# Masks laid into the score banks by ScalarE and VectorE, three pairs of banks, and statistics spread over the loop

## Time and profile before

| | |
|---|---|
| Time, median of 3 runs | 558.53 us (557.37 to 559.1) |
| The profiled execution: its own time, and its span | 557.49 us, 555.7 us |
| TensorE busy | 511.4 us (92%) |
| VectorE busy | 409.1 us (74%) |
| GpSimd busy | 377.6 us (68%) |
| ScalarE busy | 318.3 us (57%) |
| The first `scores` | starts at 23.96 us |
| The first `transpose_max` (line 1115) | starts at 34.25 us |
| The last `transpose_max` | starts at 378.67 us |
| Mean granted TensorE clock | 0.945 |

### The profile page before, as it was taken

One profiled execution on the slowest core, in us unless ns is written; L12 is line 12 of the kernel. 1 busy time (PEld: TensorE's weight loads), 2 busy tenths in 40 slices (PEclk: granted clock), 3 DMA queues, 4 the chain that ended last, 5 costly groups with the idle time before them and its releaser, 6 DMA issues.

```text
span 555.7 us, 19805 instructions
## 1 busy us (share of the span) xinstructions
PE 511.4 (92%) x6899; PEld 414.2 (75%) x6900; DVE 409.1 (74%) x1373; ACT 318.3 (57%) x750; POOL 377.6 (68%) x865
## 2 busy tenths in 40 slices
PE   3778999999999999999999999998898999999990
PEld 1346777877777777777777777776747999999990
DVE  3368666688898888887776766776667888888970
ACT  1415556666566657575666566455207777777760
POOL 8774365667878777778788787776621666665663
PEclk8757999999999999999999999999588999999996
DMA  6910423111111202201111112000122222222210
...
DMA packets 53445, 34.49 MB, mean 62 GB/s; under 512 B 5906, under 2 KB 50782, under 8 KB 53360
## 3 DMA queue, kind: packets, MB, share of 16 engines
...
## 4 chain that ended last, share of the span: by engine, by line
PE 48%; POOL 25%; issue 11%; DVE 10%; ACT 2%; DMA 1%; POOLq 1%; ACTq 0%; DVEq 0%
POOL rows L456 5%; PE PS L1107 5%; PE PS L1390 4%; POOL out L492 4%; PE PS L1124 4%; PE PS L1394 4%; PE PS L1152 3%; PE PS L1137 3%; PE PS L1371 3%; PE PS L1378 3%; PE PS L1064 3%; DVE nm L572 3%; PE PS L1094 3%; POOL vm L413 3%; PE PS L1161 2%
## 5 line engine op out<-in xcount | busy, mean ns | idle before, releaser
L572 DVE TENSOR_REDUCE nm<-PS 128x8 f32<-128x616 f32 x128 | 102.0, 797 | 52.3 <-PE PS L1107 48.9
L1124 PE MATMUL PS<-xT,kbd 32*117 32x128 f32 x1536 | 120.0, 288 | 0.0
L936 ACT ACTIVATE shared<-PS 117x768 f32<-117x768 f32 x128 | 104.1, 813 | 13.6 <-PE PS L1137 11.3
L1107 PE MATMUL PS<-kbd,xT 32*128 32x308 f32 x512 | 104.5, 485 | 0.0
L492 POOL DMA_INDIRECT out<-res,tok x72 | 70.9, 984 | 40.4 <-POOL tok L489 28.6
L1124 PEld LDWEIGHTS PS<-xT,kbd 32*117 32x117 f32 x1536 | 94.3, 179 | 0.1
L456 POOL DMA_INDIRECT rows<-X,pos_i x64 | 66.1, 1033 | 14.4 <-issue 9.5
L1137 PEld LDWEIGHTS PS<-moving,pairsel 128*117 128x117 bf16 x768 | 63.7, 140 | 3.7 <-issue 0.9
L1137 PE MATMUL PS<-moving,pairsel 128*117 128x128 bf16 x768 | 65.4, 222 | 0.1
L1107 PEld LDWEIGHTS PS<-kbd,xT 32*128 32x128 f32 x512 | 39.5, 188 | 33.8 <-issue 33.3
L1094 PE MATMUL PS<-maskneg,identb 128*128 128x308 bf16 x256 | 56.0, 301 | 5.2 <-DVE nm L572 5.1
...
## 6 DMA issues: line engine op xcount, KB each, us to landing
...
out<-res,tok POOLq DMA_INDIRECT x72
...
```

The lines of the kernel that those rows point to most:

```text
L572: nc.vector.tensor_reduce(nm[:, b % 2, 2 * u * GH:2 * (u + 1) * GH].rearrange("p (g i) -> p g i", g=2), PS[:, 0:2, 0:GK].rearrange("p g (i ...
L936: nc.scalar.activation(PT[:, b % 2, 2 * u:2 * u + 2, :], PS[0:CR, 2 + 2 * u:4 + 2 * u, 0:CH * P], ACT.Exp, scale=float(1.0 / np.sqrt(HD))) ...
L1107: ins = nc.tensor.matmul(PS[:, v, 0:GK].rearrange("p (i k) -> p i k", k=SK), xT[r, q % 2, j * P:(j + 1) * P], keys_of(kbd[r, q % 2, j]), s ...
L1124: nc.tensor.matmul(PS[0:CR, 2 + g, c * P:(c + 1) * P], kbd[r, q % 2, j, c * CR:(c + 1) * CR], xT[r, q % 2, j * P:(j + 1) * P], start=c == ...
```

## The change

- `put_mask` is gone. The mask is written into the score banks as a copy: by ScalarE for first halves (`seed_mask` after `exps(t-1, 1)`, for batch t+1) and by VectorE for second halves (`seed_mask` after `take_max(t, 0)`, for batch t). The scores add onto what lies there. `scores` waits for `seeded` where `put_mask` waited for `max_ready`.
- Half h = 2b + u now has the pair of banks 2 (h mod 3), so pairs 0/1, 2/3 and 4/5 go round. The transposed scores of a half go into a pair whose scores have been read (`pairs_at`), the exponential reads them, and then the mask of half h + 3 may be laid there. The transposed maximum goes into columns 384 to 511 of such a bank. `transpose_max` no longer waits for `exp_done`.
- The transposed scores are formed on 128 partitions, not 117 (weights of 128 columns; `kbd` is 11 columns wider), so that TensorE has written every place onto which scores are added later. Ahead of the loop six `keep_busy` products open banks 0 to 5, and one opens bank 4 again.
- Statistics: 4 + 4 batches ahead of the loop, 5, 5 and 6 in iterations 0, 1 and 2, and 4 in each of the iterations 3 to 12. Those of batch 8 and later take their inverse root on GpSimd (`inverse_roots`, 8 batches at a time in iterations 3, 5, 6, 7, 10, 11, 14) and not by ScalarE's square root; `scales` follows in iterations 4, 9 and 17. VectorE starts on Wq and Wk without waiting for the mask to land.
- QUANT is 18, not 14, and the loads of the experts' weights are started one group later. Three of x's loads go behind the second group of the context.
- GpSimd builds `pairsel` from two small tiles by four additions, between the first `expand_keys`; `mark_owners` and `build_lists` come later (after `split_max(0)` and `split_max(4)`).
- The transposes of Wo and of the router's weights and the product Wv Wo are moved from ahead of the loop into its iterations 0 and 1.

```diff
-QUANT = 14
+QUANT = 18
+EARLY = (8, 13, 18, 24)
+ROOTS = {3: 8, 5: 16, 6: 24, 7: 32, 10: 40, 11: 48, 14: 56}
...
+KW = CC - CR + P
+
+
+def scores_at(h):
+
+    return 2 * (h % 3)
+
+
+def pairs_at(b, u):
+
+    return 2 * ((2 * b + 2 - u) % 3)
...
-            for b in range(QB):
-                expand_keys(b)
-            step(nc.gpsimd.memset(pairsel[:], 0.0))
+            step(nc.gpsimd.memset(maskrow[:], 0.0))
+            step(nc.gpsimd.affine_select(out=maskrow[:], in_=maskrow[:], compare_op=ALU.not_equal, fill=1.0,
+                                         base=-MR, pattern=[[-1, SK]], channel_multiplier=1))
+            step(nc.gpsimd.memset(headpart[:], 0.0))
+            for part_ in range(PARTS):
+                step(nc.gpsimd.affine_select(out=headpart[:], in_=headpart[:], compare_op=ALU.not_equal, fill=1.0,
+                                             base=-part_ * H, pattern=[[-1, H]], channel_multiplier=1))
+            step(nc.gpsimd.memset(pairsel[:, :, 0:GH * SP].rearrange("p g (i k) -> p g i k", k=SP)[:, :, :, SK], 0.0))
+            step(nc.gpsimd.memset(pairsel[:, :, GH * SP:CC], 0.0))
+            expand_keys(0)
+            expand_keys(1)
             for g in range(G):
-                pairs = keys_of(pairsel[:, g])
-                step(nc.gpsimd.affine_select(out=pairs, in_=pairs, compare_op=ALU.not_equal, fill=1.0,
-                                             base=-MR, pattern=[[0, GH], [-1, SK]], channel_multiplier=1))
-                for part_ in range(PARTS):
-                    step(nc.gpsimd.affine_select(out=pairs, in_=pairs, compare_op=ALU.not_equal, fill=1.0,
-                                                 base=-part_ * H - g * GH, pattern=[[-1, GH], [0, SK]], channel_multiplier=1))
+                if g == 2:
+                    expand_keys(2)
+                step(nc.gpsimd.tensor_tensor(keys_of(pairsel[:, g]), maskrow[:].unsqueeze(1).broadcast_to([P, GH, SK]),
+                                             headpart[:, g * GH:(g + 1) * GH].unsqueeze(2).broadcast_to([P, GH, SK]), ALU.add))
             pool.sem_inc(pairs_ready, 1)
-            for c in range(CH):
-                for i in (c, c + 1):
-                    for s in range(2):
-                        step(nc.gpsimd.tensor_copy(vm[:, s, c, :, SUM_AT[i]], own[:, c, i * HD:i * HD + 1].broadcast_to([CR, G])))
+            expand_keys(3)
+
+            def mark_owners():
...
+            def inverse_roots(of, nth):
+                pool.wait_ge(var_ready, nth)
+                nc.gpsimd.tensor_tensor(rstd[:, of], ve[:, of], mhalf[:, 0:1].broadcast_to([P, of.stop - of.start]),
+                                        ALU.pow).then_inc(inv_ready, 1)
+
             for b in range(B + 1):
                 q, j = b // QB, b % QB
+                if b in ROOTS:
+                    inverse_roots(slice(ROOTS[b], ROOTS[b] + 8), 2 + ROOTS[b] // 8)
...
-            dve.wait_ge(qk_in, 16 * 3)
+            dve.wait_ge(qk_in, 16 * 2)
             for bd, w in ((wq_bd, wq8), (wk_bd, wk8)):
                 ins = nc.vector.tensor_tensor(bd[:], w[:].unsqueeze(1).broadcast_to([P, H, HD]), headsel[:], ALU.mult)
             step(ins, qk_ready)
+            gather_stats(0, 4)
+            add_eps(slice(0, 4), 1)
+            dve.wait_ge(mask_in, 16)
             step(nc.vector.tensor_scalar(maskneg[:], mask_i[:].unsqueeze(1).broadcast_to([P, GH, SK]), 0.0, MASKED,
-                                         ALU.is_equal, ALU.mult))
+                                         ALU.is_equal, ALU.mult), maskneg_ready)
             step(nc.vector.tensor_scalar(maskpad[:, MR:P], mask_i[:], 0.0, MASKED, ALU.is_equal, ALU.mult), maskpad_ready)
 
             step(nc.vector.tensor_reduce(seen[:], maskneg[:, 0], AX.X, ALU.max))
             step(nc.vector.tensor_scalar(seen[:], seen[:], 0.0, None, ALU.is_equal))
-            gather_stats(0, FIRST)
-            add_eps(slice(0, FIRST), 1)
             dve.wait_ge(MT_psum, 1)
-            step(nc.vector.tensor_copy(MT[:], PS[:, 1, 0:P]), MT_copied)
-            scales(slice(0, FIRST), 1)
+            step(nc.vector.tensor_copy(MT[:], PS[:, 7, 0:P]), MT_copied)
+            scales(slice(0, 4), 1)
+            gather_stats(4, 8)
+            add_eps(slice(4, 8), 2)
             dve.wait_ge(w_in, 16 * N_W)
             step(nc.vector.tensor_tensor(wv_bd[:], wv8[:].unsqueeze(1).broadcast_to([P, H, HD]), headsel[:], ALU.mult))
...
+            scales(slice(4, 8), 2)
+
...
+            def seed_mask(h):
+
+                if h == 3:
+                    dve.wait_ge(max_ready, 1)
+                else:
+                    dve.wait_ge(exp_done, h - 3)
+                nc.vector.tensor_copy(PS[:, scores_at(h):scores_at(h) + 2, 0:GK],
+                                      maskneg[:].rearrange("p i k -> p (i k)").unsqueeze(1).broadcast_to([P, 2, GK])).then_inc(seeded[1], 1)
...
+                if 1 <= t < B:
+                    seed_mask(2 * t + 1)
...
-                if t < 4:
-                    gather_stats(FIRST * (2 * t + 1), min(FIRST * (2 * t + 3), B))
-                if t == 3:
-                    add_eps(slice(FIRST, B), 2)
+                if t < 3:
+                    gather_stats(EARLY[t], EARLY[t + 1])
+                if 3 <= t < 13:
+                    gather_stats(24 + 4 * (t - 3), 28 + 4 * (t - 3))
+                if t == 2:
+                    add_eps(slice(8, 16), 3)
+                    add_eps(slice(16, 24), 4)
+                if t in (4, 6, 8, 10, 12):
+                    add_eps(slice(16 + 4 * (t - 2), 24 + 4 * (t - 2)), 5 + (t - 4) // 2)
                 if t == 4:
-                    scales(slice(FIRST, B), 2)
+                    scales(slice(8, 16), 3)
+                if t == 9:
+                    scales(slice(16, 32), 4)
+                if t == 17:
+                    scales(slice(32, B), 5)
                 if t < B:
                     take_max(t, 1)
+                if t == 0:
+                    keep_late_weights()
+                if t == 1:
+                    keep_wvo()
...
+            def seed_mask(h):
+
+                if h < 3:
+                    act.wait_ge(banks_opened, 1 if h < 2 else 2)
+                    act.wait_ge(maskneg_ready, 1)
+                else:
+                    act.wait_ge(exp_done, h - 3)
+                nc.scalar.copy(PS[:, scores_at(h):scores_at(h) + 2, 0:GK],
+                               maskneg[:].rearrange("p i k -> p (i k)").unsqueeze(1).broadcast_to([P, 2, GK])).then_inc(seeded[h % 2], 1)
...
-                if t == 3:
-                    roots_of(slice(FIRST, B), 2)
+                if 1 <= t < B - 1:
+                    seed_mask(2 * t + 2)
...
-            def put_mask(b, u):
-
-                ge(pe, max_ready, 2 * b + u)
-                for v in range(2):
-                    nc.tensor.matmul(PS[:, v, 0:GK], identb[:], maskneg[:].rearrange("p i k -> p (i k)"),
-                                     start=True, stop=False)
...
+                pe.wait_ge(seeded[u], b + 1)
                 for v in range(2):
                     g = 2 * u + v
                     r = slice(g * GR, (g + 1) * GR)
-                    ins = nc.tensor.matmul(PS[:, v, 0:GK].rearrange("p (i k) -> p i k", k=SK), xT[r, q % 2, j * P:(j + 1) * P],
-                                           keys_of(kbd[r, q % 2, j]), start=False, stop=True, tile_position=(g * GR, 0))
+                    ins = nc.tensor.matmul(PS[:, scores_at(2 * b + u) + v, 0:GK].rearrange("p (i k) -> p i k", k=SK), xT[r, q % 2, j * P:(j + 1) * P],
+                                           keys_of(kbd[r, q % 2, j]), start=False, stop=True, tile_position=(g * GR, 0),
+                                           skip_group_check=True)
...
-                ge(pe, exp_done, 2 * b)
-                nc.tensor.matmul(PS[0:PARTS * H, 2, 0:P], nm3[:], identb[:], start=True, stop=True).then_inc(nmT_psum, 1)
+                nc.tensor.matmul(PS[0:PARTS * H, pairs_at(b, 1), CH * P:BANK], nm3[:], identb[:], start=False, stop=True,
+                                 skip_group_check=True).then_inc(nmT_psum, 1)
 
             def scores_of_pairs(b, u):
 
                 q, j = b // QB, b % QB
-                ge(pe, exp_done, 2 * b - u)
+                pe.wait_ge(max_ready, min(2 * b + 3 - u, 2 * B))
                 for c in range(CH):
                     for g in (2 * u, 2 * u + 1):
                         r = slice(g * GR, (g + 1) * GR)
-                        nc.tensor.matmul(PS[0:CR, 2 + g, c * P:(c + 1) * P],
-                                         kbd[r, q % 2, j, c * CR:(c + 1) * CR],
+                        nc.tensor.matmul(PS[:, pairs_at(b, u) + g - 2 * u, c * P:(c + 1) * P],
+                                         kbd[r, q % 2, j, c * CR:c * CR + P],
...
-                    put_mask(t, 0)
                     scores(t, 0)
+                if t == 0:
+                    transpose_ctx(1)
...
-                    put_mask(t, 1)
                     scores(t, 1)
```

(4 more changed lines are left out.)

124 lines of the change are left out of this document (75 added, 49 removed).

## The result

The changed kernel is slower: 565.47 us (median of 4, 563.86 to 567.65) against 557.95 us (median of 4, 556.08 to 559.10) on the same chip, a ratio of 1.0138, 95% interval 1.0104 to 1.0172. The forecast was 549 us and its range ended at 562. A second set of runs of it (after_again) gave 566.18 us, 1.0147 (1.0122 to 1.0172). Every ratio here is to the kernel before on the same chip, and an execution over 1.5% above the fastest of its kernel is left out of it.

The account below looks back on a forecast made before the run. Loop iterations looked bound by TensorE, sharing the path with VectorE and GpSimd once rows are stored. Stage terms -10.9 - 4.5 + 4.0 - 1.6 + 7.1 - 3.7 gave -9.6 us: forecast 549 us, range 537 to 562.

Parts of the forecast that it names:

- The price of a copy: VectorE's mask copy into PSUM: 0.80 us, 0.70 us of it engine time, with bounds of 0.40 and 0.80.
- A: Start, up to batch 0's transposed maximum: earlier first scores cut 34.25 us to 23.4, a gain of 10.9.
- E: Transposed maxima of batches 18 to 46: VectorE's total work sets 160.7 us for 153.61, a loss of 7.1.
- VectorE has room: Claim for the loop from batch 46 to 63: VectorE has waits left, so its mask copies were priced at nothing.
- F: Transposed maxima of batches 46 to 63: fewer mask products on the path, a gain of 3.7 us from 89.69.
- D: Transposed maxima of batches 13 to 18: TensorE saves 2.6 us and 1.0 is given back, a gain of 1.6.
- the forecast's own signs: Wrong in kind if TensorE waits for ScalarE's mask every fourth iteration, or batches 46 to 63 take at least 89.69 us.
- The gain of TensorE's products: Batches 46 to 63: three pairs of mask products leave the path, 0.78 us in 21.34, 3.3 us in 17 iterations.
- C: Transposed maxima of batches 5 to 13: VectorE's work of 43.2 us plus waits gives 45.3, a loss of 4.0.
- B: Transposed maxima of batches 0 to 5: fewer statistics and table loads, 28.5 us for 32.97, a gain of 4.5.
- Rival 2: ScalarE's mask behind a key copy is not hidden; TensorE loses 1.4 us in each of 14 groups: 569 us, chance 0.16.
- Rival 3: Start gains less than half, from a 1.2 GHz clock through five iterations or late x chunks: 558 us, chance 0.14.

Follow-up runs that it names:

- all_scalar: Changed kernel with ScalarE writing the second halves' masks too, VectorE none; 550.71 us, 0.9864 of the kernel before.
- no_mask: Changed kernel with no engine laying a mask, scores starting on their own and maxima unmasked; 551.94 us, 0.9918 of the kernel before.
- mask_by_pe: Changed kernel with TensorE laying the masks again by two products per half, into the rotating banks; 548.95 us, 0.9886 of the kernel before.
- after_and_products: Changed kernel with TensorE laying masks again by unneeded products in the first 13 batches; 563.38 us, 1.0074 of the kernel before.
- scalar_and_stats_behind: Changed kernel with ScalarE writing every mask and the loop's statistics moved behind copy_sums; 547.98 us, 0.9847 of the kernel before.
- products_early_again: Second set of runs of products_early, unaltered; 542.65 us, 0.9741 of the kernel before.
- lists_later: As mask_by_pe, with the loop's statistics behind copy_sums and GpSimd's lists behind batch 9, not 4; 547.41 us, 0.9815 of the kernel before.
- products_early: As scalar_and_stats_behind, with TensorE laying masks again by unneeded products in the first 13 batches; 544.79 us, 0.9716 of the kernel before.

## Why the prediction was wrong

**What came true.** The price of a copy was right (794 ns measured, 0.80 taken), and so was A (24.09 for 23.4). E was right in size and in kind (161.16 for 160.7): VectorE waits 3.8 us there in all, its total work sets the stage, and all_scalar gives back 7.1 where 7.1 was the forecast loss. ScalarE's share was misread (60 to 64% of the loop stages from M5 on in the earlier trace rows, not 64 to 67), which changed no term.

**The step that failed first is "VectorE has room" in F**, with the copies priced at nothing there and in D. That VectorE's mask is there before TensorE's second scores held: TensorE waits 0.2 us for it in all of F. But I looked only at who waits for the mask, and not at what stands behind the copy on VectorE: the residual, for which `weigh` waits, and the second maximum, for which the split waits. F cost 3.0 us by that, and D 1.5 (all_scalar), where the forecast had nothing. By the forecast's own signs F was wrong in kind: M46 to M63 is 91.53 us, not shorter than 89.69.

**The gain of TensorE's products was not there, and that is the second half of the same step.** Of 3.7 us in F 1.1 came (before 89.69; no_mask 88.67, all_scalar 88.55). The forecast took three pairs of products out of the chain of the earlier trace rows and left the chain as it was. The chain of all_scalar over four batches shows what took their place:

```profile
288.84 0.21 POOL nm L455
...
301.44 0.24 PE PS L1201
...
306.18 0.04 DVE nm L621
...
309.01 0.79 DVE nm L621
...
309.85 0.21 POOL nm L455
```

GpSimd has the path for 12.60 us, TensorE for 4.74 and VectorE for 3.67, 21.01 in all. Before, it was 12.63, 7.85 and 0.86, 21.34 in all. TensorE's part fell by 3.1 us, but VectorE's own work between the two maxima of a batch (ranks, residual, its statistics) took 2.8 us of that, since the second maximum stands behind it. In the changed kernel VectorE's part is 4.14 and the four batches take 21.65 us. So the copy costs 0.64 us once in four batches and not in each, 2.7 us in 17 iterations, of the 3.0 measured. In D 0.9 came where 2.6 were forecast (27.87 in mask_by_pe, 26.97 in all_scalar), and the 1.0 that D was to give back is there (26.83 before against 27.87).

**C: +4.2.** About half is the clock, which the forecast took to be 1.00 there: C is 49.54 at 0.90, 47.34 at 0.96 (after_again) and 47.19 at 1.00 (after_and_products). The other 1.9 are place again: VectorE's work was summed to 43.2 us (39.87 measured), but the statistics stand ahead of the second maximum, which alone costs 2.6 us or more. With them behind `copy_sums` the same work fits in 43.63. The rule of the forecast for C, that VectorE's total work sets it, did not hold either: with eight copies (5.6 us) fewer on VectorE, C is 43.11 at 0.96 (scalar_and_stats_behind) and 42.44 at 1.00 (products_early_again). That its sum came within 2 us of the stage at full clock is in part luck.

**B: +5.4, most of it the clock.** The forecast named a stretch at 1.2 GHz but gave it the size of before. At 1.00 the changed kernel's B is 30.26 with the useless products in it, so 3.6 of the 5.4 us are the granted clock; 1.8 stay. They are a term that the sum did not have: GpSimd's lists behind the split of batch 4. The fifth iteration was put at 5.4 us and takes 7.28 in that profile (7.26 in the changed kernel's own); lists_later shows 2.1 us of it to be the lists. The first four sum to 22.98 where 23.1 were put, though not one by one.

**The rivals.** Rival 2 named the right sign and the wrong place: TensorE's waits for ScalarE's mask in E and F come every fourth iteration, as it said, but are 4.7 us (7 times) and 1.6 us (3 times) in all, not 1.4 us each, and all_scalar, with twice ScalarE's copies, is the faster kernel. Rival 3, the clock, was right in kind for B (33.88; it said 35) and was priced as if nothing else could go wrong at once. Its counter-argument, a TensorE that waits less, fell: TensorE is busy for 89% of B (30.19 of 33.88 us) and was for 90%.

**Open:** which of the two, the residual or the second maximum, carries more of the copy's cost outside F was not separated. D is 29.97 us at a clock of 0.94 in after_again and 31.14 at 0.89 in after_and_products, against 28.45 at 1.00. So the lower level can fall there as well, and what brings it then, no run shows. Nor is it shown why it costs 0.25 us per microsecond on the mean (below) and more in B of products_early (5.63 us for 13.5 us at 1.2 GHz).
